# One row maximum for two head pairs, newly found step lists, and weight work of the opening on GpSimd, in a gated cross-attention block

## The chip, the cores and the metric

The kernel runs on one core of a Trainium2 chip. The metric is the device time of one execution in microseconds, the median of several runs of the whole program, from the first load to the last store. The engines are called TensorE (PE in the profile), VectorE (DVE), ScalarE (ACT), GpSimd (POOL) and SyncE (SP, which only issues transfers).

## What is computed

One layer with two parts, for a batch of 32. The queries are 112 rows of 256 numbers, the context is 375 rows of 256. The first part is cross-attention with 16 heads of 64; its result is projected, multiplied by tanh of a gate and added to x. The second part is a feed-forward net with three-valued weights and activations rounded to 255 levels, again gated and added.

```python
x  = x + tanh(g_x) * attn(ctx, layernorm(x), fside, ...)   # q = ln(x) @ Wq * (1+scale) + shift; k, v = ln(ctx) @ Wkv
                                                           # softmax(q k^T / 8) v, then @ Wout
x  = x + tanh(g_f) * ffn(layernorm(x))                     # bitlinear 256->1024, gelu, bitlinear 1024->256
# bitlinear: rows scaled by 127/max|row| after rmsnorm and rounded; weight w -> round(w / mean|w|) in {-1, 0, 1}
```

## The kernel before, in words

All sizes are float32 outside. Inside, every float32 product is made of three float16 products (the helper `three`, L844 to L846): each operand is split into a high part and a rest, and high by high, high by rest and rest by high are summed in PSUM.

**Steps and lists.** The work is cut into named steps, and each engine runs its steps in an order that is written out: a list for the first batches (FIRST), a list that is repeated once per batch (ORDER, each name with an offset of batches), and a list for the last ones (LAST). Nothing but semaphores ties the engines together; a step that waits holds up everything behind it in its own engine's list.

**Attention steps of a batch b.** Z0, Z1 and ZX (L918, L922) turn the normalised context and queries on TensorE; ZF/ZXF (ScalarE, L581, L589) and ZS/ZXS (GpSimd, L460 to L469) make their two parts. K0 to K7 are the keys (six matmuls of 375 columns each), V00 to V12 the values (six of 512), Q0 and Q1 the queries (24 of 112 each). Each of these, and OO, WO, F0, F1, F2, takes the next of three `work` banks of PSUM in turn, and waits until that bank has been emptied. K and V are emptied by a ScalarE step (KH, VH, L530) and then a VectorE step (KL, VL, L681); Q by four ScalarE instructions (QF, L574) and then split on GpSimd (QS, L454, L456).

**Scores.** The 16 heads are 8 pairs. S0 to S7 (L863) write the scores of one pair into two of the four banks of `ps_s`: pair p uses banks 2(p%2) and 2(p%2)+1. S of pair g waits until the exponentials of pair g-2 are done. M0 to M7 (VectorE, L759) take the negated row maximum of the pair, E0 to E7 (ScalarE, L608, two instructions) the exponentials into `prob`. E of pair g also waits until the rest of pair g-2 was made (`p_lo`), since `prob` has two places. PH (ScalarE L618 for pairs 0, 2, 4, 6; VectorE L766 for 1, 3, 5, 7) makes the high part, PL (GpSimd, L448) the rest, T (SyncE) turns both by a DMA into `pt`, one of six places, and A0 to A7 (TensorE) multiply by the values. N0 to N3 (VectorE, L688, L690) divide; OO0 and OO1 (L927) turn the result, OH and OT split it.

**Token steps.** Every 128 rows of the output (28 tiles for 32 batches, so one batch in eight has none) go through WO, X1, XST, SC1, XR, XQ, F0, F1, HE0, HE1, GE, SQ, HMX, SC2, HR, HQ, F2, YE, ST.

**Opening.** Weights are loaded once and split: WKH, WQH, WVH, WOH on ScalarE (L521) and WKL, WQL, WVL, WOL on VectorE (L650). WOH needs the load of `wout`. AS0 and AS1 (VectorE, L662) sum the absolute values of the two feed-forward weights, SUM and WM finish the means, RW0 and RW1 (ScalarE, L526) scale and round, TN0 and TN1 (VectorE, `ternary`, L675 and L677) clip to three values. LNW(b) (ScalarE, L598, L599) is the normalisation of batch b that Z0(b) waits for. OH0(0) and WO wait for the split of `wout`; F0(0) waits for TN0, F2 and GE of the first tile for TN1.

Of the kernel before, what the change touches and what calls it, by code (L numbers as in the profile page):

```python
# [1007 lines left out]
```

## Time and profile before

| what | value |
|---|---|
| median of 3 runs | 1119.94 us (1119.65 to 1120.71) |
| the profiled execution's own time | 1121.15 us |
| its span in the profile | 1119.3 us |
| TensorE busy | 1068.0 us, 95% |
| TensorE weight load busy | 733.5 us, 66% |
| VectorE busy | 946.4 us, 85% |
| ScalarE busy | 970.7 us, 87% |
| GpSimd busy | 772.1 us, 70% |

The busy time of an engine is the time in which at least one of its instructions runs. Matmuls overlap in TensorE, and their ends are modelled, so that a short wait between two of them can lie under the modelled end of the first; such waits show better as idle time of the weight load (PEld). All rows of waits give the time, the number of times and the longest. The profiled execution took 1.85 us more than its span, which is start and end around the profiled instructions.

### The profile page before, as it was taken

What the parts mean: (1) busy time and instruction counts of PE and PEld (TensorE: products, weight loads), DVE (VectorE), ACT (ScalarE), POOL (GpSimd) and SP (SyncE); (2) the same over time, 40 slices, a digit from 0 to 9 for tenths busy, and PEclk for the clock granted to TensorE, in tenths of its full rate; (3) what the DMA queues carried; (4) which work ended last, traced back from release to release, by engine and by line L of the source; (5) the groups of instructions that cost most, each with busy time, mean ns of one, the idle gap of its engine ahead of it and who ended that gap; (6) DMA issues with size and microseconds to landing.
All of it is one profiled execution on the core that took longest, in us unless ns stands there. A gap on an engine that the chain in (4) does not pass through costs nothing.

```text
span 1119.3 us, 32134 instructions
## 1 busy us (share of the span) xinstructions
PE 1068.0 (95%) x11910; PEld 733.5 (66%) x11910; DVE 946.4 (85%) x2112; ACT 970.7 (87%) x1865; POOL 772.1 (69%) x837
## 2 busy tenths in 40 slices
PE   3999999999999999999999999999999999999994
PEld 2566767666766766776766676776666676666662
DVE  5897788988888888888898878898888888888884
ACT  5788799999999799999999979999999988999762
POOL 3566676777667678767677766777766767777552
PEclk9899999999999999999999999999999999999996
DMA  8456667757667865687775575775667686654550
GB/s 272 86 109 107 101 106 122 123 97 126 115 114 118 133 104 101 123 115 110 134 119 99 120 118 99 122 127 104 115 119 120 109 137 112 97 124 106 112 114 24
DMA packets 408153, 129.08 MB, mean 115 GB/s; under 512 B 389792, under 2 KB 402848, under 8 KB 408000
## 3 DMA queue, kind: packets, MB, share of 16 engines
q1 hardware_dynamic: 408000, 127.03, 64.1%
q8 instruction: 98, 1.61, 0.6%
q14 instruction: 55, 0.45, 0.1%
HBM read 26.71 MB, written 3.67 MB: 27 GB/s over the span
## 4 chain that ended last, share of the span: by engine, by line
PE 78%; ACT 9%; DMA 5%; issue 3%; DVE 2%; POOL 1%; POOLq 0%; DVEq 0%; SPq 0%; ACTq 0%
PE work L844 16%; PE work L846 16%; PE work L845 16%; PE ps_s L863 11%; DMA pt<-pn 4%; PE ps_o L844 3%; PE ps_o L846 3%; PE ps_o L845 3%; PE work L927 3%; ACT prob L608 2%; ACT q_f L574 2%; ACT L608 2%; PE work L956 2%; PE work L918 2%; PE work L965 2%
## 5 line engine op out<-in xcount | busy, mean ns | idle before, releaser
L448 POOL TENSOR_TENSOR pn<-prob,pn 112x750 f16<-112x750 f32 x256 | 400.2, 1569 | 117.5 <-ACT pn L618 97.8
L608 ACT ACTIVATE prob<-ps_s,neg_max 112x375 f32<-112x375 f32 x512 | 265.1, 573 | 10.5 <-DVE neg_max L759 7.5
L759 DVE TENSOR_REDUCE neg_max<-ps_s 112x2 f32<-112x750 f32 x256 | 237.6, 929 | 21.6 <-PE ps_s L863 21.5
L844 PE MATMUL ps_o<-v_h,pt 128*128 128x65 f16 (+1 forms) x1536 | 166.5, 194 | 9.1 <-DMA pt<-pn 7.6
L844 PE MATMUL work<-z,wkv_h 128*128 128x375 f16 x512 | 168.4, 329 | 2.7 <-POOL z L469 2.5
L681 DVE SCALAR_TENSOR_TENSOR k_l<-work,k_h 128x375 f16<-128x375 f32 x256 | 136.4, 541 | 38.4 <-ACT k_h L530 38.3
L530 ACT ACTIVATE k_h<-work 128x375 f16<-128x375 f32 x256 | 121.4, 488 | 53.4 <-PE work L846 48.6
L846 PE MATMUL work<-z,wkv_l 128*128 128x375 f16 x512 | 167.2, 327 | 0.0
L845 PE MATMUL work<-z,wkv_h 128*128 128x375 f16 x512 | 166.8, 326 | 0.0
L845 PE MATMUL ps_o<-v_l,pt 128*128 128x65 f16 (+1 forms) x1536 | 166.3, 192 | 0.0
L846 PE MATMUL ps_o<-v_h,pt 128*128 128x65 f16 (+1 forms) x1536 | 166.3, 193 | 0.0
L844 PEld LDWEIGHTS ps_o<-v_h,pt 128*128 128x128 f16 (+1 forms) x1536 | 143.4, 97 | 22.5 <-DMA pt<-pn 10.4
L845 PEld LDWEIGHTS ps_o<-v_l,pt 128*128 128x128 f16 (+1 forms) x1536 | 142.6, 98 | 9.5
L844 PE MATMUL work<-wkv_h,z 128*128 128x512 f16 (+1 forms) x384 | 146.8, 382 | 1.2 <-DVE k_l L681 1.2
L846 PE MATMUL work<-wkv_h,z 128*128 128x512 f16 (+1 forms) x384 | 145.5, 379 | 0.0
L845 PE MATMUL work<-wkv_l,z 128*128 128x512 f16 (+1 forms) x384 | 145.4, 379 | 0.0
L846 PEld LDWEIGHTS ps_o<-v_h,pt 128*128 128x128 f16 (+1 forms) x1536 | 142.5, 97 | 0.0
L681 DVE SCALAR_TENSOR_TENSOR v_l<-work,v_h 128x512 f16<-128x512 f32 (+1 forms) x192 | 128.3, 681 | 7.1 <-ACT v_h L530 6.6
L530 ACT ACTIVATE v_h<-work 128x512 f16<-128x512 f32 (+1 forms) x192 | 115.3, 601 | 11.4 <-PE work L846 9.5
L618 ACT ACTIVATE pn<-prob 112x750 f16<-112x750 f32 x128 | 107.8, 842 | 0.1
L574 ACT ACTIVATE q_f<-work,side_add,side_mul 128x112 f32<-128x112 f32 x256 | 93.9, 466 | 2.9 <-PE work L846 2.8
L863 PE MATMUL ps_s<-k_h,q_h 64*112 64x375 f16 x512 | 88.7, 343 | 2.2 <-ACT prob L608 1.8
(135 smaller groups left out, 2723.5 us busy)
## 6 DMA issues: line engine op xcount, KB each, us to landing
ctx_in<-in_ctx SPq DMA_DIRECT2D x32, 375.0 KB
pt<-pn SPq DMA_TRANSPOSE x256, 3.5
x_in<-in_x SPq DMA_DIRECT2D x32, 112.0 KB, 3.8
x_res<-in_x SPq DMA_DIRECT2D x28, 128.0 KB, 5.0
out<-y SPq DMA_DIRECT2D x28, 128.0 KB, 2.0
stage<-in_wkv SPq DMA_DIRECT2D x2, 1024.0 KB, 9.3
stage<-in_w SPq DMA_DIRECT2D x2, 1024.0 KB, 13.1
stage<-in_wq SPq DMA_DIRECT2D x1, 1024.0 KB, 8.2
```

Source lines behind the costliest of these rows:

```text
L448: g.tensor_tensor(buf[:, 1, :, 0:SK], prob[:, p % 2], buf[:, 0, :, 0:SK], ALU.subtract).then_inc(p_lo, 1)
L530: a.activation(dst, src, ACT.Identity, scale=1.0 / W_SCALE).then_inc(hi_done, 1)
L574: i = a.activation(q_f[:, c, :], work[:, BANK[job], m * SQ:(m + 1) * SQ], ACT.Identity, bias=add, scale=mul)
L608: i = a.activation(prob[:, p % 2, h, :], ps_s[0:SQ, 2 * (p % 2) + h, 0:SK], ACT.Exp, bias=neg_max[:, 2 * (p % 2) + h:2 * (p % 2) + h + 1])
L618: a.activation(pn[g % PBUF][:, 0, :, 0:SK], prob[:, p % 2], ACT.Identity).then_inc(p_hi_act, 1)
L681: v.scalar_tensor_tensor(out=dst, in0=src, scalar=1.0 / W_SCALE, in1=hi_part, op0=ALU.mult, op1=ALU.subtract).then_inc(evacuated[BANK[job] ...
L759: v.tensor_reduce(neg_max[:, 2 * (p % 2):2 * (p % 2) + 2], ps_s[0:SQ, 2 * (p % 2):2 * (p % 2) + 2, 0:SK], X, ALU.max, negate=True).then_in ...
L844: t_.matmul(dst, sh, mh, start=(n == 0), stop=False)
L845: t_.matmul(dst, sh, ml, start=False, stop=False)
L846: i = t_.matmul(dst, sl, mh, start=False, stop=(n == len(pairs) - 1))
L863: i = t_.matmul(ps_s[0:SQ, 2 * (p % 2) + h, 0:SK], q[r, p, :], k[r, p, :], start=(n == 0), stop=(n == 2))
L927: i = t_.transpose(w[:, m * SQ:(m + 1) * SQ], attn[:, c * P:(c + 1) * P], ident[0:SQ, 0:SQ])
```

## The change

Three things. A row maximum now covers the four banks of two pairs in one instruction: it waits for the scores of both pairs and writes all four columns of `neg_max`, and the exponentials of both pairs wait for it. So M1, M3, M5 and M7 leave VectorE's lists, and 128 reductions of 1500 elements take the place of 256 of 750. The split of `wout` (WOL) and the clipping of the feed-forward weights (TN0, TN1) move from VectorE to GpSimd, each as two instructions over 2048 elements per partition, into GpSimd's FIRST list. And all lists of all engines are written anew; each engine has the same steps but for those named. In the repeated lists S steps stand in the neighbouring pairs (S0 S1), (S2 S3), (S4 S5), (S6 S7) before and after. The LAST lists are left out below.

```diff
 ORDER["PE"] = [
-    ("V02", 0), ("V00", 0), ("S0", 0), ("S1", 0), ("V01", 0), ("A5", -1), ("Q1", 0), ("K0", 1),
-    ("S2", 0), ("S3", 0), ("OO0", -1), ("A6", -1), ("K1", 1), ("A7", -1), ("ZX", 1), ("V10", 0),
-    ("V11", 0), ("K2", 1), ("A0", 0), ("S4", 0), ("S5", 0), ("F0", -2), ("K3", 1), ("OO1", -1),
-    ("A1", 0), ("V12", 0), ("F1", -2), ("S6", 0), ("S7", 0), ("F2", -3), ("Z0", 2), ("WO", -1),
-    ("K4", 1), ("A2", 0), ("Q0", 1), ("A3", 0), ("K7", 1), ("K5", 1), ("Z1", 2), ("A4", 0),
-    ("K6", 1),
+    ("K7", 0), ("K6", 0), ("K5", 0), ("V02", 0), ("S0", 0), ("S1", 0), ("V00", 0), ("Z1", 1),
+    ("A4", -1), ("A5", -1), ("V01", 0), ("Q1", 0), ("S2", 0), ("S3", 0), ("OO0", -1), ("K0", 1),
+    ("A6", -1), ("A7", -1), ("K1", 1), ("V10", 0), ("ZX", 1), ("V11", 0), ("S4", 0), ("S5", 0),
+    ("F0", -2), ("K2", 1), ("K3", 1), ("A0", 0), ("F1", -2), ("OO1", -1), ("V12", 0), ("F2", -3),
+    ("A1", 0), ("S6", 0), ("S7", 0), ("WO", -1), ("Z0", 2), ("K4", 1), ("A2", 0), ("Q0", 1),
+    ("A3", 0),
 ]
 ORDER["ACT"] = [
-    ("PH0", 0), ("E1", 0), ("QF1", 0), ("XR", -2), ("KH0", 1), ("OH0", -1), ("E2", 0), ("KH1", 1),
-    ("ZXF", 1), ("E3", 0), ("VH10", 0), ("PH2", 0), ("VH11", 0), ("KH2", 1), ("LNW", 2), ("E4", 0),
-    ("KH3", 1), ("OH1", -1), ("E5", 0), ("VH12", 0), ("PH4", 0), ("GE", -2), ("ZF0", 2), ("SQ", -2),
-    ("KH4", 1), ("E6", 0), ("QF0", 1), ("KH7", 1), ("KH5", 1), ("PH6", 0), ("ZF1", 2), ("KH6", 1),
-    ("E7", 0), ("VH02", 1), ("HR", -2), ("VH00", 1), ("E0", 1), ("VH01", 1),
+    ("KH1", 1), ("E3", 0), ("VH10", 0), ("PH2", 0), ("VH11", 0), ("ZXF", 1), ("LNW", 2), ("KH2", 1),
+    ("KH3", 1), ("E4", 0), ("E5", 0), ("OH1", -1), ("VH12", 0), ("PH4", 0), ("GE", -2), ("SQ", -2),
+    ("ZF0", 2), ("KH4", 1), ("E6", 0), ("QF0", 1), ("KH7", 1), ("KH6", 1), ("E7", 0), ("KH5", 1),
+    ("PH6", 0), ("VH02", 1), ("HR", -2), ("VH00", 1), ("ZF1", 2), ("E0", 1), ("E1", 1), ("VH01", 1),
+    ("PH0", 1), ("XR", -1), ("QF1", 1), ("OH0", 0), ("KH0", 2), ("E2", 1),
 ]
 ORDER["DVE"] = [
-    ("KL1", 0), ("N3", -2), ("BS", 1), ("PH3", -1), ("VL10", -1), ("XTE", -3), ("VL11", -1), ("M4", -1),
-    ("KL2", 0), ("HE0", -3), ("M5", -1), ("KL3", 0), ("HTE", -4), ("OT1", -2), ("HE1", -3), ("VL12", -1),
-    ("N0", -1), ("YE", -4), ("PH5", -1), ("M6", -1), ("BA", 2), ("X1", -2), ("HMX", -3), ("KL4", 0),
-    ("XST", -2), ("N1", -1), ("KL7", 0), ("KL5", 0), ("M7", -1), ("BB", 2), ("SC2", -3), ("KL6", 0),
-    ("PH7", -1), ("M0", 0), ("VL02", 0), ("VL00", 0), ("M1", 0), ("VL01", 0), ("N2", -1), ("SC1", -2),
-    ("PH1", 0), ("M2", 0), ("KL0", 1), ("OT0", -1), ("M3", 0),
+    ("KL0", 0), ("KL1", 0), ("BS", 1), ("PH3", -1), ("XTE", -3), ("VL10", -1), ("VL11", -1), ("M4", -1),
+    ("HE0", -3), ("KL2", 0), ("KL3", 0), ("HTE", -4), ("HE1", -3), ("PH5", -1), ("OT1", -2), ("YE", -4),
+    ("N0", -1), ("VL12", -1), ("M6", -1), ("BA", 2), ("X1", -2), ("HMX", -3), ("XST", -2), ("KL4", 0),
+    ("BB", 2), ("N1", -1), ("KL7", 0), ("KL6", 0), ("SC2", -3), ("PH7", -1), ("KL5", 0), ("M0", 0),
+    ("VL02", 0), ("VL00", 0), ("SC1", -2), ("N2", -1), ("PH1", 0), ("VL01", 0), ("M2", 0), ("OT0", -1),
+    ("N3", -1),
 ]
 ORDER["POOL"] = [
-    ("XB", -2), ("HQ", -3), ("XQ", -2), ("PL1", 0), ("QS1", 0), ("LNA", 2), ("PL2", 0), ("PL3", 0),
-    ("ZXS", 1), ("PL4", 0), ("RM2", -2), ("PL5", 0), ("RM1", -1), ("QS0", 1), ("ZS0", 2), ("PL6", 0),
-    ("ZS1", 2), ("PL7", 0), ("PL0", 1),
+    ("ZS0", 1), ("RM2", -3), ("RM1", -2), ("QS0", 0), ("PL6", -1), ("PL7", -1), ("ZS1", 1), ("HQ", -3),
+    ("PL0", 0), ("XQ", -2), ("PL1", 0), ("XB", -2), ("QS1", 0), ("LNA", 2), ("PL2", 0), ("PL3", 0),
+    ("PL4", 0), ("PL5", 0), ("ZXS", 1),
 ]
 ORDER["SP"] = [
-    ("LX", 4), ("T4", 1), ("T5", 1), ("T6", 1), ("ST", -2), ("T7", 1), ("T0", 2), ("XD", 0),
-    ("HD", -1), ("T1", 2), ("LD", 5), ("T2", 2), ("RS", 1), ("T3", 2),
+    ("T1", 2), ("LD", 5), ("T2", 2), ("T3", 2), ("LX", 5), ("T4", 2), ("T5", 2), ("T6", 2),
+    ("T7", 2), ("RS", 2), ("HD", 0), ("XD", 1), ("ST", -1), ("T0", 3),
 ]
...
 FIRST["PE"] = [
-    ("Z1", 0), ("Z0", 0), ("K1", 0), ("K0", 0), ("K2", 0), ("ZX", 0), ("K4", 0), ("K3", 0),
-    ("Q0", 0), ("Z0", 1), ("K7", 0), ("K5", 0), ("K6", 0), ("Z1", 1), ("S0", 0), ("S1", 0),
-    ("V02", 0), ("V00", 0), ("K0", 1), ("Q1", 0), ("S2", 0), ("V10", 0), ("V01", 0), ("S3", 0),
-    ("ZX", 1), ("K1", 1), ("S4", 0), ("V11", 0), ("A0", 0), ("A1", 0), ("K3", 1), ("S5", 0),
...
+    ("Z0", 0), ("Z1", 0), ("ZX", 0), ("K1", 0), ("K0", 0), ("K2", 0), ("Q0", 0), ("K3", 0),
+    ("K4", 0), ("K7", 0), ("S0", 0), ("S1", 0), ("Z0", 1), ("K6", 0), ("K5", 0), ("V02", 0),
+    ("Z1", 1), ("V00", 0), ("V01", 0), ("Q1", 0), ("S2", 0), ("S3", 0), ("ZX", 1), ("K1", 1),
+    ("K0", 1), ("V10", 0), ("K2", 1), ("S4", 0), ("S5", 0), ("A0", 0), ("V11", 0), ("V12", 0),
+    ("Z0", 2), ("A1", 0), ("S6", 0), ("S7", 0), ("K3", 1), ("K4", 1), ("A2", 0), ("Q0", 1),
...
 FIRST["ACT"] = [
-    ("LNW", 0), ("WKH0", 0), ("ZF1", 0), ("ZF0", 0), ("WQH", 0), ("WKH1", 0), ("KH1", 0), ("WVH", 0),
-    ("KH0", 0), ("KH2", 0), ("ZXF", 0), ("WOH", 0), ("KH4", 0), ("KH3", 0), ("LNW", 1), ("QF0", 0),
-    ("ZF0", 1), ("KH7", 0), ("KH5", 0), ("ZF1", 1), ("KH6", 0), ("VH02", 0), ("E0", 0), ("VH00", 0),
...
+    ("LNW", 0), ("WKH0", 0), ("WKH1", 0), ("ZF0", 0), ("ZF1", 0), ("WQH", 0), ("ZXF", 0), ("WVH", 0),
+    ("KH1", 0), ("KH0", 0), ("WOH", 0), ("KH2", 0), ("QF0", 0), ("KH3", 0), ("KH4", 0), ("LNW", 1),
+    ("KH7", 0), ("ZF0", 1), ("KH6", 0), ("KH5", 0), ("VH02", 0), ("ZF1", 1), ("TNH", 0), ("E0", 0),
+    ("VH00", 0), ("E1", 0), ("VH01", 0), ("PH0", 0), ("QF1", 0), ("ZXF", 1), ("KH1", 1), ("E2", 0),
...
 FIRST["DVE"] = [
-    ("BA", 0), ("BB", 0), ("BS", 0), ("WKL0", 0), ("ZS1", 0), ("WQL", 0), ("WKL1", 0), ("KL1", 0),
-    ("BA", 1), ("KL0", 0), ("BB", 1), ("KL2", 0), ("BS", 1), ("WVL", 0), ("KL4", 0), ("KL3", 0),
-    ("WOL", 0), ("KL7", 0), ("KL5", 0), ("AS0", 0), ("KL6", 0), ("M0", 0), ("BA", 2), ("VL02", 0),
-    ("M1", 0), ("VL00", 0), ("KL0", 1), ("BB", 2), ("PH1", 0), ("M2", 0), ("VL10", 0), ("M3", 0),
...
+    ("BA", 0), ("BB", 0), ("BS", 0), ("WKL0", 0), ("ZS1", 0), ("WKL1", 0), ("WQL", 0), ("BA", 1),
+    ("KL1", 0), ("KL0", 0), ("BB", 1), ("BS", 1), ("KL2", 0), ("WVL", 0), ("KL4", 0), ("KL3", 0),
+    ("KL7", 0), ("AS1", 0), ("KL6", 0), ("KL5", 0), ("M0", 0), ("VL02", 0), ("AS0", 0), ("VL00", 0),
+    ("VL01", 0), ("PH1", 0), ("M2", 0), ("BA", 2), ("KL1", 1), ("BB", 2), ("BS", 2), ("KL0", 1),
...
 FIRST["POOL"] = [
-    ("LNA", 0), ("ZS0", 0), ("ZXS", 0), ("LNA", 1), ("SD", 0), ("QS0", 0), ("ZS1", 1), ("ZS0", 1),
-    ("PL0", 0), ("PL1", 0), ("QS1", 0), ("PL2", 0), ("LNA", 2), ("PL3", 0), ("PL4", 0), ("GT", 0),
-    ("ZXS", 1), ("PL5", 0), ("QS0", 1), ("ZS0", 2), ("PL6", 0), ("ZS1", 2), ("PL7", 0), ("PL0", 1),
-    ("QS1", 1), ("PL1", 1), ("PL2", 1), ("LNA", 3), ("ZXS", 2), ("PL3", 1), ("PL4", 1), ("QS0", 2),
-    ("PL5", 1), ("ZS1", 3), ("PL6", 1), ("ZS0", 3), ("PL7", 1), ("PL0", 2),
+    ("LNA", 0), ("ZS0", 0), ("SD", 0), ("ZXS", 0), ("LNA", 1), ("QS0", 0), ("WOL", 0), ("ZS1", 1),
+    ("ZS0", 1), ("PL0", 0), ("PL1", 0), ("QS1", 0), ("GT", 0), ("LNA", 2), ("PL2", 0), ("PL3", 0),
+    ("ZXS", 1), ("PL4", 0), ("ZS0", 2), ("PL5", 0), ("QS0", 1), ("PL6", 0), ("ZS1", 2), ("PL7", 0),
+    ("TN0", 0), ("PL0", 1), ("PL1", 1), ("QS1", 1), ("LNA", 3), ("PL2", 1), ("PL3", 1), ("ZXS", 2),
+    ("TN1", 0), ("PL4", 1), ("PL5", 1),
 ]
@@ -474,7 +473,24 @@
                 pool.drain()
                 g.tensor_tensor(ln_nb[0:TP, :], ln_nm[0:TP, :], ln_rs[0:TP, :], ALU.mult).then_inc(ln_ready, 1)
 
+            def split_output_weights():
+                pool.wait_ge(hi_split[3], 1)
+                g.tensor_scalar(wout_f, wout_f, W_SCALE, 0.0, ALU.mult, ALU.add)
+                pool.drain()
+                g.tensor_tensor(wout_l[:], wout_f, wout_h[:], ALU.subtract).then_inc(lo_split[3], 1)
+
+            def ternary(n):
+                w = (w1_f, w2_f)[n]
+                pool.wait_ge(tern_rounded[n], 1)
+                g.tensor_scalar(w, w, -ROUND, 1.0, ALU.add, ALU.min)
+                pool.drain()
+                g.tensor_scalar((w1_t, w2_t)[n][:], w, -1.0, 1.0, ALU.max, ALU.min).then_inc(tern_ready[n], 1)
+
             def step(name, b):
+                if name == "WOL":
+                    split_output_weights()
+                if name in ("TN0", "TN1"):
+                    ternary(int(name[2]))
                 if name == "SD":
                     prepare_sides()
                 if name == "GT":
@@ -601,7 +617,7 @@
                 if name[0] == "E":
                     p = int(name[1])
                     g = b * PAIRS + p
-                    act.wait_ge(max_ready, g + 1)
+                    act.wait_ge(max_ready, g // 2 + 1)
                     if g >= 2:
                         act.wait_ge(p_lo, g - 1)
                     for h in range(2):
@@ -669,13 +685,6 @@
                 dve.drain()
                 v.reciprocal(w_inv[:], w_mean[:]).then_inc(mean_ready, 1)
 
-            def ternary(n):
-                w = (w1_f, w2_f)[n]
-                dve.wait_ge(tern_rounded[n], 1)
-                v.tensor_scalar(w, w, ROUND, 1.0, ALU.subtract, ALU.min)
-                dve.drain()
-                v.tensor_scalar((w1_t, w2_t)[n][:], w, -1.0, None, ALU.max).then_inc(tern_ready[n], 1)
-
             def lo(step, job, dst, src, hi_part):
                 dve.wait_ge(hi_done, HI_COUNT[step])
                 v.scalar_tensor_tensor(out=dst, in0=src, scalar=1.0 / W_SCALE, in1=hi_part,
@@ -736,15 +745,10 @@
                     split_lo(1, wq_f, wq_h, wq_l)
                 if name == "WVL":
                     split_lo(2, wkv_f[:, :, INNER:2 * INNER], wkv_h[:, :, INNER:2 * INNER], wkv_l[:, :, INNER:2 * INNER])
-                if name == "WOL":
-                    split_lo(3, wout_f.rearrange("p (a k) n -> p a (k n)", a=2), wout_h[:].rearrange("p (a k) n -> p a (k n)", a=2),
-                             wout_l[:].rearrange("p (a k) n -> p a (k n)", a=2))
                 if name in ("AS0", "AS1"):
                     sum_weight(int(name[2]))
                 if name == "WM":
                     weight_means()
-                if name in ("TN0", "TN1"):
-                    ternary(int(name[2]))
                 if name in ("VL00", "VL01", "VL02", "VL10", "VL11", "VL12"):
                     half, t = int(name[2]), int(name[3])
                     r, c = slice(0, KEYS[t][1]), slice(half * 8, half * 8 + 8)
@@ -755,8 +759,8 @@
                 if name in ("M0", "M1", "M2", "M3", "M4", "M5", "M6", "M7"):
                     p = int(name[1])
                     g = b * PAIRS + p
-                    dve.wait_ge(scored, g + 1)
-                    v.tensor_reduce(neg_max[:, 2 * (p % 2):2 * (p % 2) + 2], ps_s[0:SQ, 2 * (p % 2):2 * (p % 2) + 2, 0:SK], X, ALU.max, negate=True).then_inc(max_ready, 1)
+                    dve.wait_ge(scored, g + 2)
+                    v.tensor_reduce(neg_max[:], ps_s[0:SQ, :, 0:SK], X, ALU.max, negate=True).then_inc(max_ready, 1)
                 if name[0:2] == "PH":
                     p = int(name[2])
                     g = b * PAIRS + p
```

## Rows read from the trace of the kernel before

**Rows 1.** The head of the page, and busy time of each engine.

```profile
span 1119.3 us, 32134 instructions
PE 1068.0 (95%) x11910; PEld 733.5 (66%) x11910; DVE 946.4 (85%) x2112; ACT 970.7 (87%) x1865; POOL 772.1 (69%) x837
```

**Rows 2.** Opening, steady part, end: length, busy of PE, PEld, DVE, ACT, POOL, clock, DMA.

```profile
0.00:164.60 164.60, 141.16 (x1449) 91.71 (x1450) 126.91 (x259) 127.99 (x249) 98.44 (x128) 0.98 0.63 130
164.60:992.10 827.50, 821.04 (x9294) 569.68 (x9292) 720.16 (x1638) 752.42 (x1454) 600.32 (x633) 1.00 0.68 116
992.10:1119.30 127.20, 105.75 (x1170) 72.06 (x1168) 99.28 (x217) 90.31 (x162) 73.33 (x78) 0.90 0.44 93
```

**Rows 3.** The same for one batch with all token steps, and one without WO.

```profile
495.60:529.00 33.40, 33.33 (x377) 23.22 (x376) 29.51 (x69) 30.83 (x59) 24.41 (x27) 1.00 0.80 117
331.70:363.90 32.20, 31.07 (x354) 20.77 (x352) 27.70 (x63) 30.71 (x59) 23.88 (x26) 1.00 0.68 117
```

**Rows 4.** Waits between 140 and 980 us, of matmuls and of weight loads.

```profile
PEld ps_s L863 <- ACT prob L608: 15.9, 44, 0.4
PEld work L918 <- ACT q_f L574: 9.3, 21, 0.5
...
PE ps_o L844 <- DMA pt<-pn: 5.0, 5, 1.2
PEld work L844 <- DVE k_l L681: 3.9, 19, 0.2
```

**Rows 5.** Groups of VectorE instructions by form: busy, mean ns, idle before.

```profile
L759 DVE TENSOR_REDUCE neg_max<-ps_s 112x2 f32<-112x750 f32 x256 | 237.6, 929 | 21.6 <-PE ps_s L863 21.5
...
L662 DVE TENSOR_REDUCE w_abs<-stage 128x1 f32<-128x2048 f32 x2 | 4.5, 2274 | 0.0
L675 DVE TENSOR_SCALAR stage<-stage 128x2048 f32<-128x2048 f32 x2 | 2.8, 1375 | 0.0
...
L677 DVE TENSOR_SCALAR w_t<-stage 128x2048 f16<-128x2048 f32 x2 | 2.6, 1323 | 0.2
...
L650 DVE SCALAR_TENSOR_TENSOR wout_l<-stage,wout_h 128x1024 f16<-128x1024 f32 x2 | 2.3, 1214 | 0.0
```

**Rows 6.** TensorE's start times of two 512-column matmuls of a V step.

```profile
495.38 0.38 PE L845 MATMUL work<-wkv_l,z 128*128 128x512 f16 x1
495.59 0.38 PE L846 MATMUL work<-wkv_h,z 128*128 128x512 f16 x1
```

**Rows 7.** Groups of ScalarE: the exponentials.

```profile
L608 ACT ACTIVATE prob<-ps_s,neg_max 112x375 f32<-112x375 f32 x512 | 265.1, 573 | 10.5 <-DVE neg_max L759 7.5
```

**Rows 8.** Groups of GpSimd: two operands, and one operand.

```profile
L448 POOL TENSOR_TENSOR pn<-prob,pn 112x750 f16<-112x750 f32 x256 | 400.2, 1569 | 117.5 <-ACT pn L618 97.8
...
L510 POOL TENSOR_SCALAR stage<-stage 128x1024 f16<-128x1024 f32 x28 | 37.6, 1342 | 16.7 <-ACT stage L637 16.7
```

**Rows 9.** Opening, in order of time: TensorE's two longest idle times, and ScalarE's.

```profile
13.31 1.48 PE L918 MATMUL work<-ident,ctx_n 125*128 125x125 f32 x6 [13.31 <-ACT x_n L599]
30.40 0.86 PE L918 MATMUL work<-ident,ctx_n 125*128 125x125 f32 x3 [3.74 <-ACT x_n L599]
...
25.64 1.91 ACT L521 ACTIVATE wout_h<-stage 128x2048 f16<-128x2048 f32 x1 [1.66 <-DMA stage<-in_wout]
```

**Rows 10.** The stretch behind the second idle time; the clock is the third column from the end.

```profile
30.00:33.00 3.00, 2.60 (x10) 1.61 (x11) 1.23 (x2) 2.15 (x6) 1.20 (x2) 0.50 0.45 116
```

**Rows 11.** From S0 of batch 1 to S0 of batch 2, and ScalarE's wait in it.

```profile
64.40:99.70 35.30, 32.73 (x355) 20.60 (x352) 29.56 (x55) 29.05 (x56) 23.25 (x22) 1.00 0.55 97
...
ACT prob L608 <- DVE neg_max L759: 1.5, 1, 1.5
```

**Rows 12.** A VectorE cast beside a GpSimd subtraction; then all casts, min/median/max ns.

```profile
98.95 1.96 DVE L766 CAST pn<-prob 112x750 f16<-112x750 f32 x1 [0.31 <-ACT prob L608]
...
98.94 1.56 POOL L448 TENSOR_TENSOR pn<-prob,pn 112x750 f16<-112x750 f32 x1
...
L766 DVE CAST pn<-prob x128: 535/543/1964, 43.7 to 1079.9; 112x750 f16<-112x750 f32 x128
```

145 rows, old and new, of the table CAST_ACT are left out of this document.

## The prediction

> **What bounds the kernel now.** I read the page's head first, then the busy times by stage, then one batch by itself, then the waits. TensorE is busy in 1068.0 of 1119.3 us, ScalarE in 970.7, VectorE in 946.4 [rows 1]. That is an average over three stages. From 164.6 to 992.1 us, TensorE is busy in 821.04 of 827.5 us at full clock: 6.5 us are open. In the opening 164.6 - 141.2 = 23.4 us are open, and at the end 127.2 - 105.8 = 21.4 us [rows 2]. So most of the kernel's life is TensorE's own work, which the change doesn't touch: no matmul is added or taken away. One batch with its token steps shows how close the next engine is: of 33.4 us TensorE is busy in 33.33, ScalarE in 30.83, VectorE in 29.51, GpSimd in 24.41. A batch without WO takes 32.2 us, and there TensorE is busy in 31.07 only [rows 3]: with the long TensorE step gone, waits of the other engines come out.
>
> What a new order could still win in the steady part stands in the waits of the weight loads, which lie under the modelled ends of matmuls: 9.3 us in which a load for Z waits for the four QF instructions that empty its bank, and 3.9 us behind KL. The 15.9 us before scores are no more than 0.4 us each, in 44 of them, and I take these as the cost of going from 128-row to 64-row weights, which stays; the two waits for the turned probabilities, 5.0 us in 5 cases, look like chance in the DMA [rows 4]. So the steady part has at most 6.5 + 9.3 + 3.9 = 19.7 us to give, and some of that is counted twice.
>
> **The maximum.** A reduction of 750 elements takes 929 ns, one of 2048 takes 2274 [rows 5]: 1345/1298 = 1.04 ns an element, so 1500 elements take 929 + 750 x 1.04 = 1.71 us. For two pairs that is 0.15 us less than 2 x 0.929. Over 128 it takes 19 us from VectorE. Bounds for the new one: 1.56 us (1500 at 1.04, no fixed part) and 1.86 us (no saving). VectorE isn't what TensorE waits for, so by itself this is worth nothing on the path. What it costs is delay. Before, E0 could start 0.93 us after S0; now it waits for S1 too (three passes of 375 columns, at the pace of rows 6, 0.21 us for 512, about 0.16 each: 0.5 us) and for 1.71 us: some 1.3 us later. The queue behind it: E0 and E1 follow each other on ScalarE, 4 x 0.573 = 2.3 us at most [rows 7], and KH, VH and QF steps that empty work banks stand behind them. S2 needs E0, S3 needs E1. The chain from the end of S1 is 1.7 + 2.3 = 4.0 us. Its cover, from the new list, is V00, Z1, A4, A5, V01 and Q1: the two V steps alone are 12 x 0.21 = 2.5 us [rows 6], the A and Q steps are 60 matmuls and over 2 us more. So S2, which wants only 1.7 + 1.15 us, is clear by about 2 us and S3 by about one. The other three hand-offs have as much between them (S3 to S4: two K, two V, two A; S5 to S6: two K, F0, F1, V12, F2, two A). In SyncE's list HD and XD now stand ahead of T0 of the batch behind them, where they stood after it; T0 can wait for them, but A0 comes only after V11 of its batch, so this is nothing too. I put the delay at nothing; if the cover goes, 1 us a batch would be near 28 us.
>
> **The steady order.** What is late next is not S but a bank: with three banks, K5 now takes the one that Q0 leaves, two K steps after it, where before Z1 took it two K steps after it. That is the same 9.3 us wait again, unless ScalarE comes to QF0 earlier. S6 and S7 are now together and E6, QF0, E7 stand as before. VectorE has 0.6 us a batch more room (4 x 0.15), which helps KL to empty banks and the batches without WO, of which there are three in this part. I take back a quarter of 19.7: **-5 us**. Ends: -20 (all of it) and +12 (a wait of 0.45 us a batch, the size of the present one for QF0, at a second place).
>
> **The opening.** TensorE has two long idle times: 13.3 us until the first context is normalised, which nothing here moves, and 3.74 us until the normalised second one. The second has its root in ScalarE, which sat 1.66 us for the load of `wout` with LNW behind it [rows 9]. Behind the idle time, TensorE's granted clock is 0.50, that is 1.2 GHz and not 2.4, in 30 to 33 us [rows 10], and every matmul there takes twice as long. In the new list WOH stands ahead of KH2, QF0 and LNW(1), so the wait for the load stays; but S0 and S1 go ahead of Z0(1), and have their operands. I expect an idle time of the same size, with K4 behind it, and a start of the pipeline about 1.5 us sooner: **-1.5**, from -4 (the idle time gone) to +3 (a longer one, with its half clock).
>
> **The weight work on GpSimd.** VectorE gives up 2 x 1.21 us for WOL and 2 x 1.375 + 2 x 1.323 us for TN [rows 5], 7.8 us in all. On GpSimd a subtraction of 750 elements takes 1.57 us, so one of 2048 at most 4.3; an instruction with one operand of 1024 takes 1.34 us, so 2048 take 2.7 [rows 8]. WOL is 7.0 us, each TN 5.4: 17.8 us. WOL stands behind QS0(0) and ahead of ZS(1) and PL0, and has its cover in S0, S1, K6, K5 and four V and Q steps. TN0 stands ahead of PL0(1), TN1 ahead of PL4(1): in the stretch between S0(1) and S0(2), GpSimd goes from 23.3 to 34.0 of 35.3 us busy [rows 11], so it holds, barely. What is queued behind: PL, hence T and A, and through `p_lo` E of two pairs later. For it, the stretch loses the block of VectorE in front of a maximum (ScalarE's 1.5 us wait [rows 11]); it has 35.3 - 32.7 = 2.6 us of idle TensorE. I take **-1**, from -2.5 to +5 (one whole TN before an A).
>
> **The end.** Its last lists hold the same chain of tokens; I take 0, from -3 to +3. **Sum:** -5 - 1.5 - 1 = -7.5. Against the profiled execution: 1121.15 - 7.5 = 1113.6; it stood 1.2 us above the median of the runs, so the median is 1112.4.
>
> **A rule against the change.** A VectorE cast took 1.96 us where the median of the 128 is 0.54, and it began with a GpSimd subtraction of 1.56 us [rows 12]. The Trainium skill, page "SBUF — State Buffer", section "SBUF: two separate sides", says that VectorE in a two-port mode or with two SBUF inputs and GpSimd take a shared port pair in turns, each for a whole instruction. By that rule, the trace agrees. By it 17.8 us more of GpSimd make casts wait.
>
> **The rivals.**
> 1. *Held casts* (0.08). Casts PH1 and PH3 fall on the long GpSimd instructions: two or three waits of up to 2.7 us while their maximum stands behind, all in batches 0 and 1: +5, so 1117.4. For it: rows 12. Against: six new instructions only.
> 2. *Nothing to win* (0.15). The QF0 wait only changes its name, and the opening keeps its idle time: 1119.9 - 1 = 1119. For it: 33.33 of 33.40 us [rows 3]. The change could also fail at its own aim: if the reduction over four banks takes 1.86 us, VectorE gains nothing, and the time is this one too.
> 3. *Slower: grouped exponentials* (0.20). The place is M4, E4, E5 with KH2, KH3 around them: 2.3 us of exponentials in one piece behind a maximum 1.3 us later, so that KH and VH come late and TensorE finds no free bank. It decides from the point where a batch waits more than 0.3 us beyond now, since 0.3 x 25 = 7.5 eats the gain; at 0.6 us a batch, +15 - 2.5: 1132; at 0.45, 1129. For it: ScalarE has 2.6 us a batch left [rows 3], and VectorE's HE0, KL2, KL3, HTE and HE1 stand in one row behind M4. Against: going through that row with the durations of the trace, each bank comes free just in time.
> 4. *All of it* (0.07). The steady waits go, and the opening's: 1119.9 - 19.7 - 4 = 1096; half of it 1104.
>
> **How the numbers follow.** My case has 0.50, with 1105 to 1117. 0.2% is 2.2 us, about what a measurement can tell from no change: the line is at 1117.7 and 1122.2. Faster: case 0.50 and rival 4, 0.07, together 0.57 and 0.01 of rival 1: 0.58. Same: the rest of rival 1 and rival 2, 0.22. Slower: 0.20. The range 1102 to 1129 leaves out half of rival 4 and about half of rival 3, 0.14, and a little at the ends.
>
> **What would show it.** Right: `neg_max` 128 times at 1.7 us; VectorE near 946 - 19 - 8 = 920 us, GpSimd near 790; TensorE's busy time the same; full batches at 33.1 to 33.3 us; the open time of TensorE in the opening shorter by one to three. Wrong: a wait of scores for `prob` over 0.4 us in each batch, ScalarE waiting for `neg_max` in each batch, a batch over 33.4 us, or A(1) waiting for `pt` by more than 5 us in the opening.

## The result, and the profile after

The changed kernel takes 1138.03 us (1137.26 to 1140.81, 6 runs) where the kernel before takes 1120.34: a ratio of 1.016, 95% interval 1.015 to 1.018. It is 18 us slower, and 1112.5 was forecast, with 1129 as the upper end. The profiled execution took 1140.48 us, 2.4 us above that median; its span of 1138.7 us is 19.4 above that of before.

The page's head and the busy times, which answer to [rows 1]:

```profile
span 1138.7 us, 32006 instructions
PE 1071.4 (94%) x11910; PEld 736.2 (65%) x11910; DVE 928.4 (82%) x1978; ACT 966.4 (85%) x1865; POOL 800.1 (70%) x843
```

TensorE has the same 11910 matmuls. VectorE lost 18 us of work, GpSimd gained 28. No average tells where 19 us went. The stretches do: from the start to S0(1), to S0(2), to S0(4), to S0(29), to the end, each cut at TensorE's last matmul ahead of that S0, with the columns of [rows 2]:

```profile
0.00:63.90 63.90, 42.36 (x354) 26.57 (x354) 42.26 (x77) 43.78 (x83) 39.08 (x64) 1.00 0.65 170
63.90:112.60 48.70, 33.96 (x340) 22.02 (x338) 34.60 (x52) 28.17 (x54) 47.67 (x23) 0.86 0.37 73
112.60:181.70 69.10, 66.77 (x734) 45.57 (x732) 51.53 (x109) 54.03 (x111) 45.45 (x48) 0.95 0.61 101
181.70:1009.60 827.90, 820.85 (x9294) 569.78 (x9292) 702.87 (x1537) 748.84 (x1455) 593.53 (x632) 1.00 0.69 116
1009.60:1138.70 129.10, 107.50 (x1197) 72.26 (x1195) 97.16 (x206) 91.58 (x165) 74.38 (x78) 0.91 0.49 92
```

The same five took 64.4, 35.3 [rows 11], 64.9, 827.5 and 127.2 us before [rows 2]. So the differences are -0.5, +13.4, +4.2, +0.4 and +1.9 us. The loss is batch 1 and the two batches behind it; 1.1 us of the 4.2 are a wait of S0(2) itself, for queries that GpSimd had still to split. In batch 1 GpSimd is busy in 47.67 of 48.70 us and TensorE in 34.0 only, at a mean granted clock of 0.86 where it was 1.00 before. What GpSimd does there, in order of time:

```profile
68.35 7.11 POOL L485 TENSOR_SCALAR stage<-stage 128x2048 f32<-128x2048 f32 x1
75.61 7.18 POOL L487 TENSOR_SCALAR w_t<-stage 128x2048 f16<-128x2048 f32 x1 [0.15 <-issue]
82.77 3.07 POOL L447 TENSOR_TENSOR pn<-prob,pn 112x750 f16<-112x750 f32 x2
...
93.22 7.09 POOL L485 TENSOR_SCALAR stage<-stage 128x2048 f32<-128x2048 f32 x1
100.46 7.17 POOL L487 TENSOR_SCALAR w_t<-stage 128x2048 f16<-128x2048 f32 x1 [0.15 <-issue]
```

Each clipping instruction takes 7.1 us. I had put it at 2.7. Two of them are a block of 14.4 us, and PL0(1) starts behind it, at 82.8 us. ScalarE's list stands at E2(1), which needs the place of `prob` that PL0 frees; TensorE waits for a bank and then for the turned probabilities. ScalarE's wait, and the first two of TensorE, in the rows of the instructions behind them:

```profile
84.42 1.04 ACT L624 ACTIVATE prob<-ps_s,neg_max 112x375 f32<-112x375 f32 x2 [8.94 <-POOL pn L447]
...
78.66 0.61 PE L848 MATMUL work<-wkv_h,z 128*128 128x512 f16 x1 [3.70 <-DVE stage L776]
87.75 0.23 PE L848 MATMUL ps_o<-v_h,pt 128*128 128x65 f16 x1 [4.90 <-DMA pt<-pn]
```

TensorE's granted clock falls to its lower level, 1.2 of 2.4 GHz, when it takes up work again behind these waits:

```profile
88.00:90.00 2.00, 2.00 (x25) 1.52 (x24) 1.29 (x2) 1.28 (x4) 1.86 (x3) 0.50 0.22 49
```

VectorE is held too, without a wait in its list. Two casts and even an instruction of three elements a partition run until a GpSimd block of the list above ends:

```profile
71.54 4.33 DVE L770 CAST pn<-prob 112x750 f16<-112x750 f32 x1
...
80.06 2.75 DVE L709 TENSOR_SCALAR ln_ve<-ln_mv 125x3 f32<-125x3 f32 x1
...
95.67 5.04 DVE L770 CAST pn<-prob 112x750 f16<-112x750 f32 x1 [0.38 <-ACT prob L624]
```

The first ends at 75.87 us, just after the first clipping instruction (75.46); the second at 82.81, with the end of the second (82.79); the third at 100.71, after the third (100.31). What this holds up are the steps behind the casts: TensorE waits twice for the bank that L776 (OT0 and OT1) empties, 3.70 us behind the cast at 71.54 and 4.00 us behind the one at 95.67. Its waits from 63.9 to 125 us:

```profile
PE work L848 <- DVE stage L776: 7.7, 2, 4.0
PE ps_o L848 <- DMA pt<-pn: 4.9, 1, 4.9
```

The row maximum took what was forecast, and full batches became shorter. The page's row of the maximum:

```profile
L763 DVE TENSOR_REDUCE neg_max<-ps_s 112x4 f32<-112x1500 f32 x128 | 219.5, 1715 | 23.5 <-PE ps_s L867 23.5
```

And a full batch, from the last V matmul ahead of S0(14) to that ahead of S0(15), takes 545.60 - 512.28 = 33.32 us. Before it was 33.42: from 495.59 [rows 6] to 529.01, its first row here.

```profile
529.01 0.38 PE L846 MATMUL work<-wkv_h,z 128*128 128x512 f16 x1
```

```profile
512.28 0.38 PE L850 MATMUL work<-wkv_h,z 128*119 128x512 f16 x1
...
545.60 0.38 PE L850 MATMUL work<-wkv_h,z 128*119 128x512 f16 x1
```

All 16 full batches of the steady part gain these 0.1 us, and one batch takes more than that back: the one from S0(25) to S0(26) takes 34.4 us where it took 32.2. TensorE waits in it for the turned probabilities, 1.20 us before (the first row) and 2.12 now:

```profile
885.03 0.20 PE L844 MATMUL ps_o<-v_h,pt 128*128 128x65 f16 x1 [1.20 <-DMA pt<-pn]
```

```profile
902.92 0.20 PE L848 MATMUL ps_o<-v_h,pt 128*128 128x65 f16 x1 [2.12 <-DMA pt<-pn]
```

### The profile page after: what moved, and what is told of

Same layout as the page of the kernel before. It is cut to its first block, busy times and chain, and to the rows that moved or that the text cites. A ratio compares the mean times of both kernels' runs of the same rounds, so it can differ in the third digit from the quotient of the medians.

```text
span 1138.7 us, 32006 instructions
## 1 busy us (share of the span) xinstructions
PE 1071.4 (94%) x11910; PEld 736.2 (65%) x11910; DVE 928.4 (82%) x1978; ACT 966.4 (85%) x1865; POOL 800.1 (70%) x843
## 4 chain that ended last, share of the span: by engine, by line
PE 65%; ACT 11%; POOL 7%; issue 5%; DMA 5%; POOLq 4%; DVE 2%; DVEq 0%; SPq 0%; ACTq 0%
PE work L848 14%; PE work L850 13%; PE work L849 13%; PE ps_s L867 9%; DMA pt<-pn 4%; ACT prob L624 3%; POOL pn L447 3%; PE ps_o L848 3%; PE ps_o L850 3%; PE ps_o L849 3%; ACT L624 2%; ACT q_f L590 2%; PE work L969 2%; PE work L931 2%; PE work L960 2%
## 5 line engine op out<-in xcount | busy, mean ns | idle before, releaser
L624 ACT ACTIVATE prob<-ps_s,neg_max 112x375 f32<-112x375 f32 x512 | 259.3, 582 | 18.2 <-POOL pn L447 14.6
L763 DVE TENSOR_REDUCE neg_max<-ps_s 112x4 f32<-112x1500 f32 x128 | 219.5, 1715 | 23.5 <-PE ps_s L867 23.5
L848 PE MATMUL ps_o<-v_h,pt 128*128 128x65 f16 (+1 forms) x1536 | 161.6, 195 | 12.4 <-DMA pt<-pn 10.6
L849 PE MATMUL ps_o<-v_l,pt 128*128 128x65 f16 (+1 forms) x1536 | 161.5, 193 | 0.0
L850 PE MATMUL ps_o<-v_h,pt 128*128 128x65 f16 (+1 forms) x1536 | 161.4, 193 | 0.0
L546 ACT ACTIVATE v_h<-work 128x512 f16<-128x512 f32 (+1 forms) x192 | 117.9, 615 | 39.1 <-PE work L850 39.0
L770 DVE CAST pn<-prob 112x750 f16<-112x750 f32 x128 | 92.1, 720 | 26.6 <-ACT prob L624 26.4
```

Of the source, the lines that this page charges most:

```text
L546: a.activation(dst, src, ACT.Identity, scale=1.0 / W_SCALE).then_inc(hi_done, 1)
L624: i = a.activation(prob[:, p % 2, h, :], ps_s[0:SQ, 2 * (p % 2) + h, 0:SK], ACT.Exp, bias=neg_max[:, 2 * (p % 2) + h:2 * (p % 2) + h + 1])
L763: v.tensor_reduce(neg_max[:], ps_s[0:SQ, :, 0:SK], X, ALU.max, negate=True).then_inc(max_ready, 1)
L770: v.tensor_copy(pn[g % PBUF][:, 0, :, 0:SK], prob[:, p % 2]).then_inc(p_hi, 1)
L848: t_.matmul(dst, sh, mh, start=(n == 0), stop=False)
L849: t_.matmul(dst, sh, ml, start=False, stop=False)
```

## The experiments

**Theory A:** the clipping costs 7.1 us an instruction on GpSimd and everything behind it comes late. **Rival B:** the new order of batch 1, with its paired exponentials, starves TensorE. **Rival C:** any instruction of that size is slow at that place.

### The clipping back on VectorE

```diff
-    ("TN0", 0), ("PL0", 1), ("PL1", 1), ("QS1", 1), ("LNA", 3), ("PL2", 1), ("PL3", 1), ("ZXS", 2),
-    ("TN1", 0), ("PL4", 1), ("PL5", 1),
+    ("PL0", 1), ("PL1", 1), ("QS1", 1), ("LNA", 3), ("PL2", 1), ("PL3", 1), ("ZXS", 2),
+    ("PL4", 1), ("PL5", 1),
...
-                pool.wait_ge(tern_rounded[n], 1)
-                g.tensor_scalar(w, w, -ROUND, 1.0, ALU.add, ALU.min)
...
+                dve.wait_ge(tern_rounded[n], 1)
+                v.tensor_scalar(w, w, ROUND, 1.0, ALU.subtract, ALU.min)
...
-    ("PH1", 1), ("M2", 1), ("N3", 0), ("OT0", 0),
+    ("PH1", 1), ("M2", 1), ("TN0", 0), ("N3", 0), ("OT0", 0),
+    ("KL0", 2), ("KL1", 2), ("BS", 3), ("PH3", 1), ("TN1", 0),
```

> The changed kernel with the clipping of the feed-forward weights (TN0, TN1) back on VectorE, TN0 behind M2(1) and TN1 behind PH3(1); the maximum, the other lists and WOL stay changed. Theory A (the four clipping instructions took 7.1 us each on GpSimd, 28.6 us in all, and everything behind them in its list came late): the 20 us lost between S0(1) and S0(3) go, 1115 to 1119 us. Rival B (the new order of batch 1 with its paired exponentials is what starves TensorE): still over 1130 us.

1125.31 us; ratio to before 1.004 (1.0025 to 1.0055). 12.7 of the 18 us are gone, and B falls: the new order with its exponentials in pairs is all still there. But 1115 to 1119 was missed by 6 us. The stretch from S0(1) to S0(2) is back at 35.6 us, where the kernel before, which also clips on VectorE, has 35.3. It shows a new wait of TensorE: V10(1) wants the bank that OT0 empties, and OT0 stands behind TN0's 1.22 and 2.42 us.

```profile
79.59 0.61 PE L849 MATMUL work<-wkv_h,z 128*128 128x512 f16 x1 [3.56 <-DVE stage L777]
```

So against before the loss is not in batch 1. The profile is 3.3 us longer than that of before, and 2.0 of it stand behind S0(29). That stretch is 1.7 to 2.2 us longer in most runs with the new lists (0.8 and 1.0 in two), and 0.3 us shorter in the run below with the old ones; its cause was not looked for.

### Multiply and add in place of min and max, on GpSimd

```diff
-                g.tensor_scalar(w, w, -ROUND, 1.0, ALU.add, ALU.min)
+                g.tensor_scalar(w, w, -ROUND, 1.0, ALU.add, ALU.mult)
...
-                g.tensor_scalar((w1_t, w2_t)[n][:], w, -1.0, 1.0, ALU.max, ALU.min)
+                g.tensor_scalar((w1_t, w2_t)[n][:], w, 1.0, 0.0, ALU.mult, ALU.add)
```

> The changed kernel with the clipping left where it is on GpSimd, but with multiply and add in place of min and max, so that the weights aren't clipped to three values; sizes, types, places and waits stay. Theory A, in its form that min and max are what is dear there: each instruction falls from 7.1 to 1.9 us, the size of WOL's first one, and the time to 1117 to 1122 us. Rival C (any GpSimd instruction on these 2048 elements is slow at this place, for its size, its tensor, or a held port): they stay near 7 us and the time near 1138 us.

1119.87 us (ratio 0.9995, 0.998 to 1.001). Same tensors, places, sizes and waits. GpSimd's groups by form:

```profile
L487 POOL TENSOR_SCALAR w_t<-stage 128x2048 f16<-128x2048 f32 x2 | 3.9, 1948 | 0.3 <-issue 0.3
L485 POOL TENSOR_SCALAR stage<-stage 128x2048 f32<-128x2048 f32 x2 | 3.8, 1900 | 0.0
```

1.9 us where it was 7.1: the price is that of min and max, and C falls. The 5.2 us an instruction, four times, is 20.8 us of GpSimd, and the time fell by 18.2. S0(1) to S0(2) is 30.8 us here, where it was 48.7.

### The kernel before with nothing but the clipping moved

```diff
-    ("VL01", 1), ("TN0", 0), ("VL02", 1), ("KL0", 2), ("TN1", 0), ("M2", 1)
+    ("VL01", 1), ("VL02", 1), ("KL0", 2), ("M2", 1)
...
-    ("PL7", 0), ("PL0", 1), ("QS1", 1), ("PL1", 1), ("PL2", 1), ("LNA", 3), ("ZXS", 2), ("PL3", 1), ("PL4", 1)
+    ("PL7", 0), ("TN0", 0), ("PL0", 1), ("QS1", 1), ("PL1", 1), ("PL2", 1), ("LNA", 3), ("ZXS", 2), ("PL3", 1), ("TN1", 0), ("PL4", 1)
```

> The kernel before, with its own lists and its own maximum, and only the clipping moved to GpSimd, ahead of PL0(1) and PL4(1). Theory A: the four instructions take about 7.1 us here too and cost most of 20 us: 1132 to 1142 us. Rival B (the new lists are at fault): at most 1124 us.

1139.64 us (ratio 1.0169, 1.0154 to 1.0184). The old lists and the old maximum with this one move are as slow as the whole change. Its stretch from S0(1) to S0(2), and the groups:

```profile
64.20:119.90 55.70, 35.65 (x353) 22.28 (x352) 31.04 (x51) 28.98 (x56) 51.73 (x27) 0.82 0.35 62
```

```profile
L482 POOL TENSOR_SCALAR w_t<-stage 128x2048 f16<-128x2048 f32 x2 | 14.4, 7177 | 0.3 <-issue 0.3
L480 POOL TENSOR_SCALAR stage<-stage 128x2048 f32<-128x2048 f32 x2 | 14.2, 7104 | 0.0
```

55.7 us for what took 35.3. TensorE has two waits in it, both for late steps of GpSimd, the rest of the probabilities and that of the queries:

```profile
PE ps_o L844 <- DMA pt<-pn: 10.3, 1, 10.3
PE ps_s L863 <- POOL q_l L456: 9.7, 1, 9.7
```

### WOL on VectorE as well

```diff
-    ("LNA", 1), ("QS0", 0), ("WOL", 0), ("ZS1", 1)
+    ("LNA", 1), ("QS0", 0), ("ZS1", 1)
...
-    ("KL3", 0), ("KL7", 0), ("AS1", 0)
+    ("KL3", 0), ("WOL", 0), ("KL7", 0), ("AS1", 0)
...
+                if name == "WOL":
+                    split_lo(3, wout_f.rearrange("p (a k) n -> p a (k n)", a=2), ...)
```

This is on top of the first run, at the place that WOL had before.

> The changed kernel with both the clipping and WOL back on VectorE (WOL behind KL3(0), where it was): the maximum and the lists alone. Theory A: WOL on GpSimd took 1.9 + 4.1 = 6.0 us with slack behind it, so this is within 1 us of the kernel with the clipping alone on VectorE, 1115 to 1120 us. Rival B: over 1130 us.

1125.29 us, against 1125.31 with WOL on GpSimd. The split of `wout` (1.9 + 4.1 us on GpSimd) costs nothing there and saves nothing here. The absolute 1115 to 1120 was missed with the first run's.

### One weight of two without min and max

```diff
+                if n == 0:
+                    g.tensor_scalar(w, w, -ROUND, 1.0, ALU.add, ALU.mult)
+                    pool.drain()
+                    g.tensor_scalar(w1_t[:], w, 1.0, 0.0, ALU.mult, ALU.add).then_inc(tern_ready[n], 1)
+                    return
```

> The changed kernel with multiply and add in place of min and max for the first feed-forward weight only (it isn't clipped to three values); the second stays as in the change. Theory A: half the block goes, GpSimd's instructions are 1.9 us for the one weight and 7.1 us for the other, and the time lies between the two, 1124 to 1132 us. If only the first block (ahead of PL0(1)) had hurt, it would be at 1117 to 1121 us.

1128.35 us (ratio 1.0061, 1.0046 to 1.0075), near the middle of 1119.9 and 1138.0. Half the block gives half the loss (8.5 us for the second weight, 9.7 for the first), so it isn't one unlucky place.

### The clip in two halves, exact again

Clipping may come ahead of the subtraction: min and max against ROUND+1 and ROUND-1 leave the same three values. VectorE has its part behind KL1(2) and PH3(1), GpSimd ahead of PL4(1) and behind PL5(1).

```diff
+                v.tensor_scalar(w, w, ROUND + 1.0, ROUND - 1.0, ALU.min, ALU.max).then_inc(tern_clipped[n], 1)
...
+                pool.wait_ge(tern_clipped[n], 1)
+                g.tensor_scalar((w1_t, w2_t)[n][:], w, -ROUND, 1.0, ALU.add, ALU.mult).then_inc(tern_ready[n], 1)
```

> The changed kernel, exact again, with the clipping in two instructions a weight: VectorE clips the still shifted values to ROUND-1 and ROUND+1 in one instruction (min and max, 1.2 us), and GpSimd takes ROUND away with add and multiply (1.9 us, the price that the run without min and max showed). Theory A: GpSimd keeps no long block and VectorE none of 2.5 us: 1115 to 1119 us, level with the run without min and max. Rival D (after the clipping on VectorE gave 1125 us: any extra work on VectorE in batch 1 costs 5 us): 1122 to 1126 us.

1119.21 us, ratio 0.9993 (0.9982 to 1.0004), not to be told from before; A as expected, D falls. Its stretches from S0(1), and a full batch of 525.75 - 492.43 = 33.32 us:

```profile
64.40:96.60 32.20, 29.12 (x340) 19.44 (x338) 26.68 (x53) 27.60 (x54) 25.49 (x22) 1.00 0.59 116
96.60:162.00 65.40, 64.10 (x733) 44.58 (x732) 51.47 (x109) 54.07 (x111) 44.04 (x46) 1.00 0.64 104
162.00:988.30 826.30, 819.37 (x9294) 568.82 (x9292) 703.52 (x1536) 749.65 (x1455) 593.43 (x632) 1.00 0.69 116
988.30:1117.40 129.10, 107.51 (x1197) 72.28 (x1195) 97.50 (x207) 91.63 (x165) 74.33 (x78) 0.91 0.48 92
```

Against before it has 3.1 us less from S0(1) to S0(2), 0.5 more from there to S0(4), 1.2 less in the steady part, and 1.9 more at the end.

Its rows also price the granted clock in the changed kernel. The same 340 matmuls of batch 1 are busy for 29.12 us here at 1.00 and for 33.96 us there at 0.86, and those up to S0(4) for 64.10 us here and 66.77 there at 0.95. So about 7.5 of the 20.2 us between the two kernels in these stretches are the slower clock behind the waits, and 12.7 us are idle time.

### The maximum as two instructions again

```diff
-                    act.wait_ge(max_ready, g // 2 + 1)
+                    act.wait_ge(max_ready, g + 1)
...
-                    dve.wait_ge(scored, g + 2)
-                    v.tensor_reduce(neg_max[:], ps_s[0:SQ, :, 0:SK], ...)
+                    for i in range(2):
+                        dve.wait_ge(scored, g + 1 + i)
+                        v.tensor_reduce(neg_max[:, 2 * i:2 * i + 2], ps_s[0:SQ, 2 * i:2 * i + 2, 0:SK], ...)
```

> The split clip as above, but the maximum again as two instructions of 750 elements one behind the other at the place of the one, E0 waiting for the first alone: 128 x 0.15 = 19 us more of VectorE. If the saved VectorE time is worth something in the new order, full batches go from 33.32 to 33.4 us or more, and the time rises by 2 to 5 us; if the delay of E0 was what hurt, it falls by as much; my reading is that neither is on the path: within 1.5 us of the split clip.

1120.56 us, ratio 1.0003 (0.9992 to 1.0014); the split clip had 0.9993 (0.9982 to 1.0004) beside it. VectorE is busy for 932.3 us in place of 921.4, and no more than 1.35 us come of it, which the intervals don't tell from nothing; full batches stay at 33.32 us. The 19 us that were expected came out as 10.9, in part since two reductions one behind the other take less than twice 0.93 us: the row of the 256 is 227.0 us here, 7.5 above that of the 128, where it was 237.6 in the kernel before. So the run shows that 11 us of VectorE are worth nothing that can be measured in these lists, and not what 19 would be.

### The whole clipping on VectorE at another place

```diff
-    ("M2", 1), ("TN0", 0), ("N3", 0), ("OT0", 0), ("KL0", 2), ("KL1", 2), ("BS", 3)
+    ("M2", 1), ("N3", 0), ("OT0", 0), ("KL0", 2), ("KL1", 2), ("TN0", 0), ("BS", 3)
```

> The changed kernel with the whole clipping on VectorE as in the first of these runs, but TN0 moved from behind M2(1) to behind KL1(2), so that OT0 and two KL, which free work banks, come first. If the 5 us of that run were V10 waiting for the bank behind TN0 (its 6 us step), they go: 1117 to 1121 us. If 5 us of VectorE work cost 5 us wherever it stands in batch 1: 1123 to 1127 us.

1124.24 us, ratio 1.0034 (1.0021 to 1.0047): 1.1 us below the first of these runs, which the intervals don't tell from nothing, and not 5. The wait for OT0 is gone, and K2(2) now waits as long for the bank that VL10 empties behind both clippings:

```profile
83.17 0.49 PE L849 MATMUL work<-z,wkv_h 128*128 128x375 f16 x1 [3.38 <-DVE v_l L689]
```

So at both places tried, 5 us of VectorE work among steps that empty banks cost TensorE a wait of 3.4 to 3.6 us; half of it, as in the split clip, had room.

### E6 into ScalarE's idle time

```diff
-    ("GE", -2), ("SQ", -2), ("ZF0", 2), ("KH4", 1), ("E6", 0), ("QF0", 1)
+    ("GE", -2), ("SQ", -2), ("E6", 0), ("ZF0", 2), ("KH4", 1), ("QF0", 1)
```

This is on the split clip. It goes for the wait for QF0's bank, which the prediction had expected to come back, and which did. Waits of the changed kernel in its steady stretch:

```profile
PEld work L848 <- ACT q_f L590: 8.4, 19, 0.5
```

ScalarE in order of time, split clip; 0.70 and 0.30 us are idle, then a table load and E6 ahead of QF0:

```profile
518.47 0.66 ACT L596 ACTIVATE zf<-work,lnb,lnw 128x375 f32<-128x375 f32 x1 [0.70 <-PE work L928]
519.43 0.49 ACT L545 ACTIVATE k_h<-work 128x375 f16<-128x375 f32 x1 [0.30 <-PE work L856]
519.94 1.28 ACT L623 ACT_TABLE_LOAD   x1
521.24 1.04 ACT L623 ACTIVATE prob<-ps_s,neg_max 112x375 f32<-112x375 f32 x2
522.16 1.45 ACT L589 ACTIVATE q_f<-work,side_add,side_mul 128x112 f32<-128x112 f32 x4
```

> The split clip, and in ScalarE's repeated list E6 ahead of ZF0 and KH4. In a full batch K5 waits about 0.25 us for the bank that QF0 empties, and QF0 stands behind a table load and E6, while ScalarE is idle for 0.7 and 0.3 us ahead of ZF0 and KH4. With E6 in that idle time, K5 shouldn't wait: full batches 33.07 us instead of 33.32, some 17 of them full: 4 us off the split clip, 1113 to 1117 us, faster than both kernels. If another bank comes late instead (K6, or Z0's), no gain: 1118 to 1121 us.

1117.38 us, ratio 0.9976 (0.9964 to 0.9988): faster than both kernels, by a hair, but 0.4 us above the range that was expected. The split clip had 0.9993 (0.9982 to 1.0004); the two intervals overlap a little, so the 1.8 us between the medians are not quite clear of the noise. The load and E6 come first now, without idle time ahead of them, and QF0 starts 520.45 - 491.72 = 28.73 us into the batch, where it was 522.16 - 492.43 = 29.73:

```profile
517.08 1.28 ACT L623 ACT_TABLE_LOAD   x1
518.38 1.04 ACT L623 ACTIVATE prob<-ps_s,neg_max 112x375 f32<-112x375 f32 x2
519.31 0.67 ACT L596 ACTIVATE zf<-work,lnb,lnw 128x375 f32<-128x375 f32 x1
519.86 0.49 ACT L545 ACTIVATE k_h<-work 128x375 f16<-128x375 f32 x1
520.45 1.45 ACT L589 ACTIVATE q_f<-work,side_add,side_mul 128x112 f32<-128x112 f32 x4
```

A full batch is 33.05 us (491.72 to 524.76 us), and the steady stretch, from the first matmul of S0(4) to that of S0(29), 823.4 us where the split clip had 826.2:

```profile
491.72 0.38 PE L856 MATMUL work<-wkv_h,z 128*119 128x512 f16 x1
...
524.76 0.38 PE L856 MATMUL work<-wkv_h,z 128*119 128x512 f16 x1
```

Batch by batch, 15 full batches gain 0.27 or 0.28 us each, 4.1 us in all. The others together lose 1.3 us, most of it in three batches at or near one without WO, which take 0.26 to 0.41 us longer (S0(9), S0(11) and S0(19) to the next). That leaves 2.8 us in the profile and 1.8 in the medians.

## Why the prediction was wrong

**The step that failed** is the term "The weight work on GpSimd", in its sentence that an instruction with one operand of 1024 takes 1.34 us, "so 2048 take 2.7", and "each TN 5.4". The row it scaled is an add and a multiply [rows 8]; the clipping is an add and a min, and a max and a min. (For add and multiply, doubling was a little too dear: 2048 elements took 1.9 us, and the same row of 1024 reads 1.04 us in the changed kernel.) The right price is 7.1 us an instruction, 14.3 a weight, 28.6 in all and not 10.8. The bounds were drawn around the length alone and not around the operation, so the upper end, +5, was no bound. With 28.6 us GpSimd can't hold in the stretch at all: 23.3 + 28.6 = 51.9 us in 35.3, where the text had 34.0. Run with multiply and add, the same instructions at the same places take 1.9 us each and the kernel 1119.9; run with min and max under the old lists, 1139.6.

**What was queued behind** was named rightly: PL, T and A, and E through the place in `prob`. The waits of 8.94 us (ScalarE) and 4.90 us (TensorE) are these; the 4.90 is just under the 5 us that the prediction had named as a sign of being wrong. Not named were the queries that GpSimd splits behind the block (1.1 us here, 9.7 in the run with the old lists) and the granted clock behind the waits (7.5 us).

**Held casts** (rival 1) was real: 4.33 and 5.04 us, where up to 2.7 had been allowed, and the 3.70 and 4.00 us that TensorE waits for OT's bank stand right behind them. With 1.9 us instructions the casts of that stretch took at most 1.17 us. The runs don't price the holding apart from the late PL, but it isn't needed for the loss: under the old lists casts were held too (3.20 us), no wait of TensorE stands behind one, and the loss is as large.

**Slower** had a chance of 0.20, but by another mechanism, with its place at M4, E4 and E5. Nothing of that came: a full batch is 33.32 us, and in the steady part no wait of scores for `prob` and none of ScalarE for `neg_max` is left among the waits, so the hand-offs from S to M to E are covered, as the step on the maximum said. Its size was right too: 1.715 us measured, 1.71 forecast. That was in part luck, since its slope came from another kind of reduction, a sum of absolute values, the same sort of step that failed for the clipping. That VectorE's time is worth nothing on the path is borne out for the 11 us that the two-maxima run put back.

**The steady order** was put at -5 us. Sixteen full batches did fall, by 0.10 us each, but the one batch behind S0(25) took 2.2 us more: the steady part rose from 827.5 to 827.9 in the changed kernel and fell to 826.3 in the split clip. So this term was too large, by 3.8 us or more. The waits for the turned probabilities were called chance in the text, but one stands in that same batch in every run: 1.1 to 1.2 us under the old lists, 1.7 to 3.0 under the new ones. Why the transfer comes late there stays open. **The opening** was -1.5: up to S0(1) it is -0.5, and TensorE's open time in it didn't get shorter (20.3 us before, 21.5 now). **The end** was 0: it is +1.9. In rival 4, half of the gain would be 1108, and not 1104. Had the clipping cost what I thought, the time would have been near the 1119.9 and 1119.2 us of the two runs without the block: no change, the number of rival 2, and not my 1112.5. It isn't rival 2 by mechanism: in those two runs batch 1 is 4.5 and 3.1 us shorter than before, a gain of which the end takes back 1.7 to 1.9.

## What to carry to other kernels

Scale a price along the length only within one operation of one engine; across operations it is a guess that can come out, as for the maximum, or be 2.6 times too low, as for the clipping. When an instruction moves to another engine, look for a row there with the same operators, and where none is, let the upper bound be a multiple and ask what a block of that length holds up. Then add the block to the busy time of the stretch in which it runs: 51.9 us of GpSimd don't fit in 35.3, though the 28.6 us in it are 2.5% of the kernel. Whether shorter pieces with the same sum would have cost less, no run here shows.

## What was not expected of the hardware

- GpSimd's two-scalar instruction over 128x2048 float32 takes 1.90 us with add and multiply and 7.10 to 7.18 us with min or max in it (0.93 against 3.5 ns an element). VectorE took a mean of 1.38 us (subtract and min) and 1.32 us (max) for the same clipping [rows 5]. One min is enough for it: add with min costs 7.10 us and max with min 7.18. A max without a min wasn't tried on GpSimd.
- VectorE instructions of three elements a partition were held until a GpSimd instruction had ended (2.75 us, the row at 80.06 us), and a cast for 5.04 us. The Trainium skill, page "SBUF — State Buffer", section "SBUF: two separate sides", says that GpSimd and VectorE, when VectorE is in a two-port mode or has two SBUF inputs, take a shared port pair in turns, one whole instruction at a time; the ends of the held instructions, 0.02 to 0.4 us behind those of GpSimd's, agree.
